# Recurrent front: the decay's inner product in columns 64 to 127 beside the mixer's second half, and keys projected a stage sooner

## The chip, the core and the metric

The kernel runs on one core of a Trainium2 chip. The metric is the device time of one launch in microseconds. A core has TensorE (matrix products into the accumulator memory PSUM), VectorE, ScalarE and GpSimd (elementwise work) and SyncE, which issues the transfers. Each has its own instruction queue and runs it in order; semaphores tie them together.

## The reference, cut to what matters

Four layers run one after the other on `x` of 4 samples x 512 tokens x 512 features, all in float32: a grouped attention over a context, a transformer block with self and cross attention and an MLP, and two recurrent layers (2 and 3) of one form. The change is in the first part of the recurrent layers:

```python
xa = _ln(x, ln1_w, ln1_b)
sx = concatenate([state[:, 1:2] - xa[:, :1], xa[:, :-1] - xa[:, 1:]], axis=1)
xxx = tanh((xa + sx * maa_x) @ maa_w1).reshape(b, l, 5, 32)     # the mixer: 512 -> 5*32
xxx = einsum('blfd,fde->blfe', xxx, maa_w2)                     # the mixings: 5 times 32 -> 512
xm = xa[:, :, None] + sx[:, :, None] * (maa_stack + xxx)
xk, xw, xv, xr, xg = (xm[:, :, j] for j in range(5))
w = exp(-exp(time_decay + tanh(xw @ td_w1) @ td_w2))            # the decay: 512 -> 64 -> 512
r, k, v = xr @ Wr.T, xk @ Wk.T, xv @ Wv.T
g = silu(xg @ Wg.T)
```

Then comes a recurrence over tokens (`s = k v + w s`), a group norm, an output product, and a feed-forward part.

## The kernel before

A loop runs over the four samples; all four layers of one sample are one body, each engine with a queue written out by hand. Features or tokens are tiled in four chunks of 128 (`C = 4`), tokens are 512 to a row. A recurrent layer has a front, which is what the reference's lines above say, then four rounds over the head groups (`hg`), then the output product and the feed-forward part. So there are eight fronts in a launch, two per sample.

The front on TensorE is in `pe_rwkv`. Its products are:

- `mixer(part, fc)` (L838): the mixer's product over input chunk `fc`. Part 0 gives 128 outputs (the tanh inputs of k, w, v, r, 32 each) into PSUM bank 0; part 1 gives the last 32 (g) into partitions 0 to 31 of bank 1.
- `decay_in(fc, mixed)` (L847): the decay's inner product, 64 outputs into bank 2. It is fed twice into the same sum, first by `xa` (`mixed=False`), then by `sx * (maa_w + xxx)` (`mixed=True`), so that xa needs not be added to the mixed w.
- `mixing(name, c)` (L858): one chunk of a 96-row product (32 values as high part, low part and high part again, in the format fp32r) for one of w, k, r, v, g. It writes into one of three PSUM banks, which mixings, decays and others take in turn (`take`): each use waits until the use three before it has been emptied.
- `project(0, name, fcs)` (L369): the projection of the first head group from mixed k, r or v, into the fixed banks 3, 7 and 2 (`FIRST`).
- the decay's outer product (L890): 64 rows to 128 outputs, four chunks, each into a bank of the three.

A product of float32 is recorded as two passes, one of fp32r as one.

The other engines follow the same order of names. ScalarE (`act_rwkv`) makes three tanh instructions per name w, k, r, v (L1363, L1364, L1366), then `tdh`, the tanh of the decay's inner product (L1386), then the three for g, then copies the first keys out of bank 3 (`kT`, L1375), and then makes two exponentials for each decay chunk (L1392, which empties the bank, and L1396). VectorE (`dve_rwkv`) empties each mixing with one instruction (L1126), adds `xa` to the last chunk of k, r and v (L1132), and makes the low part of each name's tanh (`z_low`, L1136); the low part for g comes after the last v. GpSimd adds `xa` to the other chunks (L1510), and later takes powers of the decay (L1520).

The weights come in blocks of 1 MB into three slots. A block may be loaded when its slot's block has been used for the last time. The block `small` holds the mixer's and both decay matrices and is free when the last L890 is done; the block of the values' weights goes into its slot (SyncE, `load_weights`, L278).

Of the kernel before, what the change touches and what calls it, by code (L numbers as in the profile page):

```python
# [16 lines left out]
ACT = mybir.ActivationFunctionType  # L17
# [4 lines left out]
C = H // P  # L22
# [26 lines left out]
SMALL_MAA, SMALL_TD1, SMALL_TD2 = 0, C * 160, C * 224  # L49
# [46 lines left out]
def build(nc, a, known, samples=B):  # L96
# [69 lines left out]
    tdh, over = place('tdh', [64, L], over)  # L166
# [46 lines left out]
    with ExitStack() as stack:  # L213
        ps = stack.enter_context(nc.psum_tensor('ps', [P, 8, 512], F32))
# [614 lines left out]
        def pe_rwkv(pe, l):  # L829
# [5 lines left out]
            def mixer(part, fc):  # L835
                n0, rows_ = ((0, 128), (128, 32))[part]
                pe.wait_ge(*dve_done.when('xin', l, fc))
                m = nc.tensor.matmul(ps[0:rows_, part, :], small[:, SMALL_MAA + fc * 160 + n0:SMALL_MAA + fc * 160 + n0 + rows_],  # L838
                                     mix[:, 1, fc, :], start=(fc == 0), stop=(fc == C - 1))
                if fc == C - 1:  # L840
                    m.then_inc(*tile_ready.reach('z', l, part))

            def decay_in(fc, mixed):
                src = mix[:, MIX_AT['w'], fc, :] if mixed else xa[:, fc, 1:L + 1]
                if mixed:
                    pe.wait_ge(*dve_emptied.when('mix', l, 'w', fc))
                m = nc.tensor.matmul(ps[0:64, 2, :], small[:, SMALL_TD1 + fc * 64:SMALL_TD1 + (fc + 1) * 64], src,  # L847
                                     start=(fc == 0 and not mixed), stop=(fc == C - 1 and mixed))
                if fc == C - 1 and mixed:
                    m.then_inc(*tile_ready.reach('td', l))  # L850

            def mixing(name, c):
                f = MIX_ROW[name]
                if c == 0:
                    pe.wait_ge(*dve_done.when('z_lo', l, name))
                    pe.wait_ge(*(act_emptied.when('z', l, int(f == 4)) if name in 'vg' else act_done.when('z_hi2', l, name)))
                tile = take(pe, 'mix', l, name, c)
                nc.tensor.matmul(tile, MIX_W[l][0:96, f * H + c * P:f * H + (c + 1) * P], zstack[0:96, f, :],  # L858
                                 start=True, stop=True).then_inc(*tile_ready.reach('mix', l, name, c))
# [8 lines left out]

            for fc in range(C):
                mixer(0, fc)  # L870
            decay_in(0, False)
            decay_in(1, False)
            pe.wait_ge(*(pool_done if l == 2 else dve_done).when('mix_w', l))
            for c in range(3):
                mixing('w', c)
            decay_in(2, False)
            mixing('w', 3)
            decay_in(3, False)
            for c in range(C):
                mixing('k', c)  # L880
                decay_in(c, True)
            for c in range(C):
                mixing('r', c)
                mixer(1, c)
            for c in range(C):
                mixing('v', c)
                project(0, 'k', (c,))
            pe.wait_ge(*act_emptied.when('td', l))
            for c in range(C):
                nc.tensor.matmul(take(pe, 'decay', l, c), small[0:64, SMALL_TD2 + c * P:SMALL_TD2 + (c + 1) * P], tdh[:, :],  # L890
                                 start=True, stop=True).then_inc(*tile_ready.reach('decay', l, c))
            for c in range(C):
# [460 lines left out]
        def act_rwkv(act, l):  # L1353
# [29 lines left out]
            for name in 'wkrv':  # L1383
                mixer_in(name)
            act.wait_ge(*tile_ready.when('td', l))
            nc.scalar.activation(tdh[:, :], ps[0:64, 2, :], ACT.Tanh).then_inc(*act_emptied.reach('td', l))  # L1386
            mixer_in('g')
            heads_in(0, 'k')
            for c in range(C + 1):
# [512 lines left out]
```

## Time and profile before

| | |
|---|---|
| median of three runs | 4186.95 us (4186.92 to 4193.72) |
| the profiled execution | 4188.31 us |
| its span, first to last instruction | 4186.5 us |
| mean granted TensorE clock | 0.952 |
| TensorE busy (weight loads, beside it) | 3719.4 us, 89% (2267.5 us, 54%) |
| VectorE busy | 2621.0 us, 63% |
| ScalarE busy | 2154.2 us, 51% |
| GpSimd busy | 1652.4 us, 39% |
| L838 (mixer), passes in all fronts | 128 |
| L847 (decay's inner product), passes | 128 |
| L858 (mixings), passes | 160 |
| L890 (decay's outer product), passes | 64 |

Busy shares are means over stages with different limits. The start of a pass on TensorE is recorded and its end is modelled, so the distance between starts is the measure of what a pass costs. Idle time in brackets is the idle time of the engine just before an instruction, with the instruction that ended it.

### The profile page before, as it was taken

To read this page: it belongs to the slowest core of one execution; us is meant where nothing else is said; L and a number is where in the kernel's file an instruction comes from. 1 tells how busy PE (TensorE), PEld (TensorE's weight loads), DVE (VectorE), ACT (ScalarE), POOL (GpSimd) and SP (SyncE) were. 2 spreads that over 40 slices of the span, in tenths; PEclk is the share of its full clock that TensorE was granted. 3 is DMA by queue.
4 is the path that set the end of the run, shared out by engine and by line. 5 is a ranking of instruction groups with operands and counts; after the bars stand their busy time and mean duration, and the time that the engine had idled before them with its cause. 6 is when DMAs were issued, how large, how long until landed. Compare 5 with 4: busy or idle time off the path is not lost. (4 is left out here: it accounts for less than half of the span.)

```text
span 4186.5 us, 66406 instructions
## 1 busy us (share of the span) xinstructions
PE 3719.4 (89%) x24448; PEld 2267.5 (54%) x24448; DVE 2621.0 (63%) x5691; ACT 2154.2 (51%) x4272; POOL 1652.4 (39%) x1849
## 2 busy tenths in 40 slices
PE   7988899899888989989888888998988888899898
PEld 4544565546554456554655445656465454565555
DVE  5765746666576564665657656467666765645766
ACT  5655733434666573343466657334346665733433
POOL 4554442232454454223245445422324544542232
PEclk9999999999999999999999999999999999999999
DMA  4032221102204122110220412211022032221102
GB/s 137 15 103 67 78 78 40 62 21 101 76 15 123 49 84 70 39 64 21 101 76 15 121 53 82 70 42 60 22 101 78 20 117 55 78 70 42 60 32 101
DMA packets 94558, 276.11 MB, mean 66 GB/s; under 512 B 25472, under 2 KB 25984, under 8 KB 73088
## 3 DMA queue, kind: packets, MB, share of 16 engines
q1 hardware_dynamic: 94208, 271.58, 20.2%
q8 instruction: 202, 3.31, 0.3%
q14 instruction: 148, 1.21, 0.1%
HBM read 201.24 MB, written 4.19 MB: 49 GB/s over the span
## 5 line engine op out<-in xcount | busy, mean ns | idle before, releaser
L805 POOL TENSOR_SCALAR probs<-probs,row_inv 128x512 f32<-128x512 f32 x1024 | 696.0, 696 | 635.1 <-DVE row_inv L720 635.1
L664 ACT ACTIVATE probs<-probs,row_max 128x512 f32<-128x512 f32 x1024 | 733.4, 725 | 132.1 <-DVE row_max L736 131.2
L559 PE MATMUL ps<-ident,probs 128*128 128x128 f32 x4096 | 606.5, 289 | 172.9 <-ACT pT L658 146.5
L559 PEld LDWEIGHTS ps<-ident,probs 128*128 128x128 f32 x4096 | 477.0, 146 | 383.0 <-ACT pT L658 211.4
L658 ACT ACTIVATE pT<-ps 128x512 f32<-128x512 f32 x768 | 430.1, 602 | 107.2 <-PE ps L559 106.5
L369 PE MATMUL ps<-mix,wring 128*128 128x512 f32 x1024 | 471.0, 596 | 3.8 <-DMA wring<-in_blocks_dram 3.8
L534 PE MATMUL ps<-kstack,qstack 96*128 96x512 f32 (+1 forms) x1024 | 380.5, 467 | 16.2 <-DMA qstack<-hi 7.1
L736 DVE CUSTOM_DVE_ANT_0 probs<-ps,maskA 128x512 f32<-128x512 f32 x512 | 329.3, 681 | 42.6 <-PE ps L534 42.6
L736 DVE CUSTOM_DVE_ANT_0 probs<-ps,neg 128x512 f32<-128x512 f32 x512 | 340.6, 685 | 8.9
L369 PEld LDWEIGHTS ps<-mix,wring 128*128 128x128 f32 x1024 | 191.2, 190 | 198.9 <-issue 178.8
L1535 POOL TENSOR_TENSOR hinv<-hvar,minus_half 128x32 f32<-128x32 f32 x24 | 146.3, 6094 | 376.8 <-DVE hvar L1255 376.8
L550 PE MATMUL ps<-pT,v 128*32 128x512 f32 x2048 | 244.6, 599 | 0.0
L369 PE MATMUL ps<-srcT,wring 128*128 128x512 f32 x512 | 238.5, 609 | 0.2
L534 PEld LDWEIGHTS ps<-kstack,qstack 96*128 96x128 f32 (+1 forms) x1024 | 177.1, 194 | 108.4 <-issue 44.1
L409 POOL TENSOR_SCALAR varep<-moments 128x1 f32<-128x1 f32 x128 | 43.0, 336 | 482.1 <-DVE moments L388 481.1
L329 POOL TENSOR_TENSOR mlp_w<-wring,mlp_w 128x2048 fp32r<-128x2048 f32 x32 | 149.5, 4672 | 194.2 <-ACT mlp_w L324 194.2
L421 PE MATMUL ps<-ident,xn 128*128 128x128 f32 x448 | 104.8, 389 | 126.6 <-DVE xn L392 126.1
L750 DVE COPY pT<-ps 128x512 f32<-128x512 f32 x256 | 168.2, 686 | 73.2 <-PE ps L559 71.7
L664 ACT ACTIVATION_READ_ACCUMULATOR probs<-probs,row_max 128x1 f32 x1024 | 205.4, 201 | 0.0
L1689 DVE TENSOR_TENSOR hidden_lo<-hidden,hidden_hi 128x512 fp32r<-128x512 f32 x64 | 94.2, 1495 | 168.7 <-ACT hidden_hi L1656 168.7
L1510 POOL TENSOR_TENSOR mix<-mix,xa 128x512 f32<-128x512 f32 x104 | 118.6, 1160 | 171.6 <-DVE mix L1126 122.4
L743 DVE TENSOR_TENSOR ps<-ps,maskA 128x1024 f32<-128x1024 f32 x128 | 156.5, 1223 | 23.1 <-PE ps L534 22.9
(177 smaller groups left out, 7025.9 us busy)
## 6 DMA issues: line engine op xcount, KB each, us to landing
wring<-in_blocks_dram SPq DMA_DIRECT2D x151, 1024.0 KB, 5.1
qstack<-hi SPq DMA_DIRECT2D x256, 64.0 KB, 2.0
kstack<-hi SPq DMA_DIRECT2D x256, 64.0 KB, 2.0
maskA<-in_mask_dram SPq DMA_DIRECT2D x9, 1024.0 KB, 7.8
rows<-in_rows_dram SPq DMA_DIRECT2D x8, 1024.0 KB, 4.6
qstack<-hi SPq DMA_DIRECT2D x256, 32.0 KB, 2.0
qstack<-lo SPq DMA_DIRECT2D x128, 64.0 KB, 2.0
kstack<-lo SPq DMA_DIRECT2D x128, 64.0 KB, 2.0
```

The source lines that it names most:

```text
L329: nc.gpsimd.tensor_tensor(low, weights(name), high.bitcast(F32), ALU.subtract).then_inc(*pool_done.reach('wlo', name))
L369: m = nc.tensor.matmul(tile, w[:, base_ + fc * H + oc * P:base_ + fc * H + (oc + 1) * P], src[:, fc, :], start=(fc == 0), stop=(fc == C - 1))
L534: nc.tensor.matmul(ps[:, qc, :], qstack[0:A.kt, g % 2, i, qc * P:(qc + 1) * P], kstack[0:A.kt, g % 2, 0 if A.shared else i, :], start=True ...
L550: ins = nc.tensor.matmul(ps[32 * h:32 * h + 32, OBANK, :], lhs, pT[:, h, kc, :], start=(kc == 0 and first), stop=(kc == C - 1 and final))
L559: ins = nc.tensor.transpose(tile[:, qc * P:(qc + 1) * P], probs[:, m % PSLOTS, qc, kc * P:(kc + 1) * P], ident[:, :])
L658: nc.scalar.activation(pT[:, m % 4, kc, :], ps[:, ring.bank('pT', t, m, kc), :], ACT.Copy)\
L664: nc.scalar.activation(p, p, ACT.Exp, bias=row_max[:, n % PSLOTS, qc:qc + 1], scale=-1.0, accum_out=row_sum[:, n % PSLOTS, qc:qc + 1]).the ...
L736: nc.vector.tensor_tensor_reduce(out=probs[:, s, qc, :], in0=ps[:, qc, :], in1=other, scale=-1.0, scalar=3.0e38, op0=ALU.add, op1=ALU.min, ...
L743: nc.vector.tensor_tensor(ps[:, two, :], ps[:, two, :], A.mask[:, two, :], ALU.mult)\
L750: nc.vector.tensor_copy(pT[:, m % 4, kc, :], ps[:, ring.bank('pT', t, m, kc), :])\
L805: nc.gpsimd.tensor_scalar(p, p, row_inv[:, (n - 1) % PSLOTS, qc:qc + 1], 1.0, ALU.mult, ALU.mult)\
L1535: nc.gpsimd.tensor_tensor(hinv[:, :, :], hvar[:, :, :], minus_half[:, :].rearrange('p (a b) -> p a b', b=HEADS), ALU.pow).then_inc(*pool_d ...
```

## The change

`decay_in` writes its 64 outputs to partitions 64 to 127 of bank 2, which puts the product in columns 64 to 127 of the array, where it was in columns 0 to 63. ScalarE reads them from there. The order on TensorE becomes:

- stage w: all of `mixer(1, fc)`, each followed by `decay_in(fc, False)`; then the four mixings of w with nothing between
- stage k: as it was, each mixing followed by `decay_in(c, True)`
- stage r: each mixing followed by one quarter of the first key projection (it was followed by `mixer(1, c)`)
- stage v: each mixing followed by one outer product of the decay (it was followed by a quarter of the key projection, with all outer products behind the stage); the wait for `tdh` stands behind the first v mixing
- stage g and the values' projection: as they were

The queues of VectorE, ScalarE, GpSimd and SyncE keep their order. The order in which banks are taken changes: v and decay chunks alternate.

```diff
-                m = nc.tensor.matmul(ps[0:64, 2, :], small[:, SMALL_TD1 + fc * 64:SMALL_TD1 + (fc + 1) * 64], src,
+                m = nc.tensor.matmul(ps[64:128, 2, :], small[:, SMALL_TD1 + fc * 64:SMALL_TD1 + (fc + 1) * 64], src,
                                      start=(fc == 0 and not mixed), stop=(fc == C - 1 and mixed))
...
             for fc in range(C):
                 mixer(0, fc)
-            decay_in(0, False)
-            decay_in(1, False)
+            for fc in range(C):
+                mixer(1, fc)
+                decay_in(fc, False)
             pe.wait_ge(*(pool_done if l == 2 else dve_done).when('mix_w', l))
-            for c in range(3):
+            for c in range(C):
                 mixing('w', c)
-            decay_in(2, False)
-            mixing('w', 3)
-            decay_in(3, False)
             for c in range(C):
                 mixing('k', c)
                 decay_in(c, True)
             for c in range(C):
                 mixing('r', c)
-                mixer(1, c)
+                project(0, 'k', (c,))
             for c in range(C):
                 mixing('v', c)
-                project(0, 'k', (c,))
-            pe.wait_ge(*act_emptied.when('td', l))
-            for c in range(C):
+                if c == 0:
+                    pe.wait_ge(*act_emptied.when('td', l))
                 nc.tensor.matmul(take(pe, 'decay', l, c), small[0:64, SMALL_TD2 + c * P:SMALL_TD2 + (c + 1) * P], tdh[:, :],
                                  start=True, stop=True).then_inc(*tile_ready.reach('decay', l, c))
...
-            nc.scalar.activation(tdh[:, :], ps[0:64, 2, :], ACT.Tanh).then_inc(*act_emptied.reach('td', l))
+            nc.scalar.activation(tdh[:, :], ps[64:128, 2, :], ACT.Tanh).then_inc(*act_emptied.reach('td', l))
```

## Rows read from the trace of the kernel before

**Rows 1.** Timeline of TensorE, first front: start us, us, instruction, idle.

```profile
612.77 1.93 PE L847 MATMUL ps<-xa,wring 128*64 128x512 f32 x4
614.82 0.94 PE L858 MATMUL ps<-zstack,mix_w 96*128 96x512 f32 x3
...
617.20 0.50 PE L858 MATMUL ps<-zstack,mix_w 96*128 96x512 f32 x1 [0.44 <-DVE mix L1126]
...
618.63 0.50 PE L858 MATMUL ps<-zstack,mix_w 96*128 96x512 f32 x1
...
623.37 1.07 PE L847 MATMUL ps<-mix,wring 128*64 128x512 f32 x2
624.37 0.50 PE L858 MATMUL ps<-zstack,mix_w 96*128 96x512 f32 x1
...
629.99 0.50 PE L858 MATMUL ps<-zstack,mix_w 96*128 96x512 f32 x1
...
630.79 0.80 PE L858 MATMUL ps<-zstack,mix_w 96*128 96x512 f32 x1
...
631.88 0.80 PE L858 MATMUL ps<-zstack,mix_w 96*128 96x512 f32 x1
...
633.61 1.02 PE L369 MATMUL ps<-mix,wring 128*128 128x512 f32 x2
634.57 3.88 PE L890 MATMUL ps<-tdh,wring 64*128 64x512 f32 x8
638.38 0.50 PE L858 MATMUL ps<-zstack,mix_w 96*128 96x512 f32 x1
...
641.99 1.02 PE L369 MATMUL ps<-mix,wring 128*128 128x512 f32 x2
643.58 3.70 PE L369 MATMUL ps<-mix,wring 128*128 128x512 f32 x8 [0.56 <-DMA wring<-in_blocks_dram]
```

**Rows 2.** Timeline of VectorE, first front.

```profile
616.40 2.73 DVE L1126 SCALAR_TENSOR_TENSOR mix<-ps,cols,sx 128x512 f32<-128x512 f32 x4
...
633.82 0.75 DVE L1126 SCALAR_TENSOR_TENSOR mix<-ps,cols,sx 128x512 f32<-128x512 f32 x1 [0.34 <-PE ps L858]
634.60 0.77 DVE L1132 TENSOR_TENSOR mix<-mix,xa 128x512 f32<-128x512 f32 x1
635.40 0.68 DVE L1136 TENSOR_TENSOR zstack<-z,zstack 32x512 fp32r<-32x512 f32 x1
638.91 0.75 DVE L1126 SCALAR_TENSOR_TENSOR mix<-ps,cols,sx 128x512 f32<-128x512 f32 x1 [2.83 <-PE ps L858]
```

**Rows 3.** Timeline of ScalarE, first front.

```profile
634.67 0.60 ACT L1375 ACTIVATE kT<-ps 128x512 f32<-128x512 f32 x1 [2.89 <-PE ps L369]
635.29 1.28 ACT L1392 ACT_TABLE_LOAD   x1
636.58 1.27 ACT L1392 ACTIVATE decay<-ps,cols 128x512 f32<-128x512 f32 x2
```

**Rows 4.** Windows, first and last front: length, busy of engines, clock, DMA share.

```profile
612.80:638.40 25.60, 25.05 (x58) 7.85 (x57) 17.12 (x24) 12.57 (x22) 10.23 (x9) 1.00 0.00 0
...
3971.00:3996.60 25.60, 25.03 (x58) 7.89 (x57) 17.10 (x24) 12.59 (x22) 10.23 (x9) 1.00 0.00 1
```

**Rows 5.** Chain that ended last (start us, us, what), one front; page's groups.

```profile
3766.06 3.82 PE ps L890 x8
3769.90 5.07 DMA wring<-in_blocks_dram
...
L369 PE MATMUL ps<-mix,wring 128*128 128x512 f32 x1024 | 471.0, 596 | 3.8 <-DMA wring<-in_blocks_dram 3.8
```

**Rows 6.** Timeline of TensorE in an attention: a context group, what follows.

```profile
3269.41 1.92 PE L550 MATMUL ps<-pT,v 128*32 128x512 f32 x16
3271.26 0.33 PE L559 MATMUL ps<-ident,probs 128*128 128x128 f32 x1
```

**Rows 7.** Timeline of GpSimd, first front.

```profile
620.70 3.44 POOL L1510 TENSOR_TENSOR mix<-mix,xa 128x512 f32<-128x512 f32 x3 [11.23 <-DVE mix L1126]
```

## The prediction

> **What bounds the kernel now.** I read the table of slices and the list of groups first. No engine is full: TensorE is busy for 89% of the span, and what the program waits for differs from stage to stage. The change touches one stage only, the front of the two recurrent layers (from the layer norm's transposes to the projection of values), which runs eight times: four samples, two layers. So the view to read is the timeline of TensorE over one front [rows 1], beside those of VectorE [rows 2] and ScalarE [rows 3] over the same stretch, and the table of windows that says whether the other fronts are like it. They are: in the first and in the last of the eight, TensorE is busy for 25.0 of 25.6 us at a granted clock of 1.00, with VectorE at 17.1 and ScalarE at 12.6 us, and no DMA runs [rows 4]. A front is bound by TensorE's queue as it is ordered, and what is taken off that queue counts, until a wait shows up in its place.
>
> The chain of work that ended last confirms the end of a front: four outer products of the decay (L890), then a weight load of 5.07 us, then the projection of values [rows 5]. That load brings the values' block into the slot of the small block, which is free only when the last L890 has read it. TensorE reaches the projection first: it could go on at 642.85 (641.99 plus two passes of 0.43) and starts at 643.58 [rows 1]. Over all fronts the group of projections has 3.8 us idle for this load [rows 5]. A record of a pass is 0.59 long and passes follow each other at 0.43, so 0.16 per front is hidden in that idle time: 3.8/8 + 0.16 = 0.64 us per front are lost here.
>
> **The prices on TensorE.** A float32 product of 512 columns is two passes of 0.43 us, 0.86 in all (L369 x8 takes 3.70 us with its tail) [rows 1]. From the same timeline: a turn of "one mixing, one decay input" takes (624.37 - 618.63)/4 = 1.43 us, of which the 64-column product is 1.00 (623.37 to 624.37) and the mixing 0.43. A turn of "one mixing, one mixer second half" takes (629.99 - 624.37)/4 = 1.41. A turn of "one mixing, one projection" takes only 631.88 - 630.79 = 1.09, though its product is as long [rows 1]. So 0.3 us of a turn is paid for going between full-width products and products of 64 or 32 columns.
>
> **The change part by part.** I write the first front as a schedule; its start, 612.77, stays.
>
> (1) Stage w. Removed: four decay inputs on xa alone or between the w mixings. Added: four second halves of the mixer, each followed by a decay input in other columns. What four products in disjoint columns do is seen in the attention's context: sixteen passes (eight products) of 32 columns take 3271.26 - 3269.41 = 1.85 us [rows 6], where one after another they would take 8 x 0.86 = 6.9. So disjoint columns work at the same time. No row shows a 32-column product beside a 64-column one. Bounds for a pair: 0.86 (beside each other) and 2.00 (two of the alternating ones at 1.00 [rows 1]). I take 0.86, since every row with disjoint columns is at that end. Four pairs are 3.45, with 0.1 for going back to full width: w0 at 616.3, where it was at 614.82.
>
> VectorE now ends this stage. The mixings take turns on three PSUM banks, so w3 waits until VectorE has emptied w0, and k0 until it has emptied w1. Its read begins 0.53 after a mixing starts (638.38 to 638.91) and takes 0.68 (2.73/4) [rows 1, 2]. The signal back takes 0.12 (616.40 + 0.68 to 617.20): 616.3 + 0.53 + 1.36 + 0.12 = 618.3 for k0, before 618.63. The decay inputs that used to fill this wait had cost nothing there, so this step gives 0.3 us and no more; four mixer halves are now inside it.
>
> (2) Stage k is unchanged in TensorE's order, 4 x 1.43: r0 at 624.1. The other columns cost the decay inputs nothing, and ScalarE's tanh reads 64 partitions as before.
>
> (3) Stage r pairs each mixing with a k projection. By the present v stage that is 0.80 for the first turn (629.99 to 630.79) and 1.09 for the others [rows 1], 4.07 in all, against 5.62 now: v0 at 628.2. The projection needs mixed keys a stage earlier: VectorE reads them from 616.85 + 2.73 + 0.7 = 620.3 on (r's low part stands between), GpSimd adds xa at 1.15 us each (3.44/3) [rows 7], and the last is there by 624.8, before its projection at 627.7. The keys' weights have landed: no DMA runs from 612.80 on [rows 4].
>
> (4) Stage v alternates mixings with L890. No row shows this pair. The nearest is 1.43 (64 columns); an L890 loads weights for 128 columns on each change, so I take 1.47, with 1.09 and 1.6 as bounds. The wait for `tdh`, now behind the first v mixing, costs nothing: its input ends with stage k at 624.1, four us earlier. The first L890 starts at about 628.9, behind the last k projection; v1 at 630.0, v2 at 631.45, v3 at 632.9. Three banks now turn among mixings and decays, so v2 waits for ScalarE to empty decay 0, v3 for decay 1. ScalarE: the tanh for g finds its input early and is out of the way; the last k projection starts 0.45 before v0 and takes 1.02 [rows 1], so kT starts at 628.8, then the 1.28 of its table load and 0.69 for the exponential, in the order and with the times of now [rows 3]: 628.8 + 0.6 + 1.28 + 0.69 = 631.35. That is 0.1 before v2 wants it: a cover with nothing to spare. If it is late by x, v2, v3 and g0 are late by x.
>
> (5) A new wait. VectorE reads v3 at 632.9 + 0.53 = 633.45 (now 633.82), adds xa and makes g's low part, which ends at 635.40 + 0.68 = 636.08 now, 2.26 after that read began [rows 2]: at 635.7, and g0 follows at 635.85. The last L890 ends near 634.4. Four L890 used to stand between v3 and g0 and hid this; now TensorE stands for some 1.4 us, with the projection of receptance behind it in its queue. g0 comes 638.38 - 635.85 = 2.5 us sooner.
>
> (6) Stage g is unchanged, 642.85 - 638.38 = 4.47: the projection of values may start at 640.3. The small block is free at 634.4 and the 5.07 us of the load end at 639.5, so SyncE's load is hidden and the 0.64 us is saved as well. What follows (vT, pair products, decay powers on GpSimd) moves with it: VectorE's products hang on the projection of receptance, which moves by 2.5, and reach their next TensorE user with more than 3.2 - 2.5 to spare.
>
> **Sum**: 2.5 + 0.64 = 3.15 us per front, 25.2 us for eight. The profiled execution took 4188.31 us, 1.8 more than its span; less 25.2 it is 4163.1. The median of the runs is 4186.95, 1.36 less, so I say 4161.8.
>
> **The rivals.**
>
> Rival A, the pair does not run side by side and each change of width is paid. For it: the trace pays 0.3 us per turn whenever widths alternate [rows 1], and 32 and 64 are different widths. Against it: the widths that were seen to pay share columns, and these don't. Then a pair costs 2.00, four cost 8.0 in place of 3.45, everything behind moves by 4.55, and a front is 4.55 - 3.15 = 1.4 us longer: +11.2 us, 4198.2. It decides as soon as a pair costs more than 0.86 + 3.15/4 = 1.65 us. 
>
> Rival C, side by side, but ScalarE or VectorE hands back the banks late in stage v. If decay 0 waits for the whole table load after it is ready (630.0 + 1.28 + 0.69 = 632.0), v2 is 0.6 late and so is g0: 2.55 us per front, 20.4 in all, 4166.6. Against it: the load now starts at 635.29, straight behind kT and before the decay is there [rows 3].
>
> **How the numbers follow.** The forecast, with the pairs side by side, 0.50; Rival C 0.08; Rival B 0.12; Rival A 0.30. The range takes in the forecast with cheap L890 turns (1.3 in place of 1.47 gives 0.5 us a front, 4158; with the rest of the roundings 4156) and Rival A, with 2 us of spread: 4156 to 4200. The forecast's own range is 4156 to 4168. About 0.2%, 8.4 us, is what a measurement of this kernel can tell from no change. Faster: forecast and C, 0.58. Same: B and a fifth of A, where a change of width costs less than at full width, 0.18. Slower: the rest of A, 0.24.
>
> **What the profile afterwards would show.** Step 1: L838 with 32 columns and L847 with 64 start within some 0.02 us of each other, the eight products take about 3.5 us, and k0 follows w0 by 2.0. If they start 0.43 apart or more and take 7 to 8 us, A or B holds. Steps 3 and 4: turns of 1.09 and 1.47. Step 5: a wait of VectorE's zstack in front of the first g mixing, 1 to 1.5 us. Step 6: no idle time for wring before the projection of values. I would be wrong, beyond the rivals, if the new wait in front of g0 let the granted clock fall below 1.00 inside a front, or if what follows a front did not move with it.

## The result, and the profile after

The change made the kernel slower: 4208.85 us (median of 7 runs, 4203.77 to 4227.76) against 4186.95 (7 runs beside them, 4180.48 to 4197.67), a ratio of 1.006 with a 95% interval of 1.0047 to 1.0072. The profiled execution took 4208.85 us, its span is 4207.1 and its mean granted clock 0.950. The forecast was 4161.8, so it had the sign wrong, and the range ended at 4200.

All that follows rests on one table. The start of each pass on TensorE cuts a front into stages; these are the means of the eight fronts of a profiled execution, in us. "To w0" is the time from the last pass of the mixer's first half to the first mixing of w, "end" that from the last mixing of g to the first product that transposes v.

| kernel | to w0 | w | k | r | v | g | end | sum |
|---|---|---|---|---|---|---|---|---|
| before | 2.57 | 3.82 | 5.72 | 5.61 | 8.37 | 2.98 | 6.52 | 35.58 |
| after | 8.44 | 2.09 | 5.70 | 4.07 | 7.88 | 4.36 | 5.78 | 38.31 |

A front grew by 38.31 - 35.58 = 2.73 us, eight of them by 21.8; the spans differ by 4207.1 - 4186.5 = 20.6. So the loss is as large as the growth of the fronts; some microseconds elsewhere are taken up at the end. Every stage behaved alike in all of them but stage g, which is treated below.

The timeline of TensorE in the first front of the kernel after (columns as in [rows 1]) shows what the pairs did:

```profile
613.53 1.57 PE L838 MATMUL ps<-mix,wring 128*128 128x512 f32 x3
...
615.46 1.07 PE L847 MATMUL ps<-xa,wring 128*64 128x512 f32 x2
616.47 1.05 PE L838 MATMUL ps<-mix,wring 128*32 128x512 f32 x2
617.44 1.07 PE L847 MATMUL ps<-xa,wring 128*64 128x512 f32 x2
...
621.40 1.07 PE L847 MATMUL ps<-xa,wring 128*64 128x512 f32 x2
622.40 0.97 PE L858 MATMUL ps<-zstack,mix_w 96*128 96x512 f32 x3
...
624.49 0.48 PE L858 MATMUL ps<-zstack,mix_w 96*128 96x512 f32 x1 [0.25 <-DVE mix L1123]
...
630.20 0.49 PE L858 MATMUL ps<-zstack,mix_w 96*128 96x512 f32 x1
...
634.27 0.80 PE L858 MATMUL ps<-zstack,mix_w 96*128 96x512 f32 x1
635.00 1.12 PE L887 MATMUL ps<-tdh,wring 64*128 64x512 f32 x2
636.05 0.50 PE L858 MATMUL ps<-zstack,mix_w 96*128 96x512 f32 x1
...
637.53 0.49 PE L858 MATMUL ps<-zstack,mix_w 96*128 96x512 f32 x1
...
639.44 1.12 PE L887 MATMUL ps<-tdh,wring 64*128 64x512 f32 x2
642.15 0.50 PE L858 MATMUL ps<-zstack,mix_w 96*128 96x512 f32 x1 [1.58 <-DVE zstack L1133]
642.48 1.87 PE L369 MATMUL ps<-mix,wring 128*128 128x512 f32 x2
643.37 1.42 PE L858 MATMUL ps<-zstack,mix_w 96*128 96x512 f32 x1
...
646.79 0.80 PE L858 MATMUL ps<-zstack,mix_w 96*128 96x512 f32 x1
647.43 4.46 PE L369 MATMUL ps<-mix,wring 128*128 128x512 f32 x10
```

The 64-column product and the 32-column product never share a row or a start. They follow each other at 1.01 and 0.97 us, so a pair takes 617.44 - 615.46 = 1.98, and the mixings of w begin at 622.40. Behind them the rest of the schedule is nearly as forecast, up to the wait of 1.58 us in front of the first mixing of g. Behind that wait stands something new: a pass of L858 of 1.42 us, and a whole stage of 646.79 - 642.15 = 4.64 us where the same instructions took 2.98.

The windows over stage g (length, busy of TensorE, its weight loads, VectorE, ScalarE and GpSimd, granted clock, DMA share, GB/s) of the first, second, sixth and eighth front say why:

```profile
642.15:646.80 4.65, 4.65 (x10) 2.35 (x10) 1.77 (x3) 0.18 (x1) 0.10 (x1) 0.63 0.47 194
869.03:874.70 5.67, 5.67 (x9) 2.84 (x10) 2.08 (x3) 0.17 (x1) 0.09 (x1) 0.51 0.41 168
...
2965.30:2968.30 3.00, 3.00 (x10) 1.66 (x10) 1.78 (x3) 0.18 (x1) 0.10 (x1) 1.00 0.75 311
...
4013.41:4016.40 2.99, 2.99 (x10) 1.66 (x10) 1.77 (x3) 0.18 (x1) 0.10 (x1) 1.00 0.79 326
```

TensorE is busy throughout, with the same work, and the granted clock is 0.63 and 0.51 in the long ones and 1.00 in the short ones. It fell to 1.2 GHz, half of full speed, for most of stage g in six of the eight fronts, and cost 1.66 us in five of them and 2.70 in the second.

### The profile page after: what moved, and what is told of

It reads as the page before. It is cut to its first block and busy times, and to the rows that moved or that the text cites. A ratio compares the mean times of both kernels' runs of the same rounds, so it can differ in the third digit from the quotient of the medians.

```text
span 4207.1 us, 66406 instructions
## 1 busy us (share of the span) xinstructions
PE 3734.0 (89%) x24448; PEld 2270.7 (54%) x24448; DVE 2623.0 (62%) x5691; ACT 2155.6 (51%) x4272; POOL 1655.9 (39%) x1849
## 3 DMA queue, kind: packets, MB, share of 16 engines
q8 instruction: 202, 3.31, 0.3%
```

## The experiments

Two questions stood open: what a pair costs and why, and what the wait in front of g does. A third came up on the way: TensorE's stops in the recurrence, which moved whenever instructions were added. Each run's stages are gathered in one table behind the first group.

### What the pair costs

Only the width of one product decides in this run: the mixer's second half is made 64 columns wide (the 32 added outputs land in partitions that nobody reads), so that both products of a pair are of one width.

```diff
-                n0, rows_ = ((0, 128), (128, 32))[part]
+                n0, rows_ = ((0, 128), (128, 64))[part]
```

> The changed kernel with one edit: the mixer's second half takes 64 columns of weights in place of 32 (columns 0 to 63 of the array; the upper 32 results are never read). Both products of a pair are then 64 wide, in columns 0 to 63 and 64 to 127, with their banks and operands as they were. Theory M (what keeps a pair apart is that 32 and 64 columns are two widths, and each change of width drains the array): the pairs run side by side, 0.86 us a pair, from the last pass of the mixer's first half to w0 8.44 falls to about 4.0 us; k0, r0, v0, g0 move with it, so 4.4 us per front, 35 us in all, near 4173 us. Theory N (a product of the mixer and one of the decay don't overlap because they read different operands or write different banks): 8.44 stays within 0.8 us of what it is (the changes of width alone are saved), at most 6 us in all.

It took 4177.75 us (12 runs), ratio 0.9979 (0.9966 to 0.9992) to before, 31.1 us below after. The timeline of TensorE, first front:

```profile
616.10 0.59 PE L838 MATMUL ps<-mix,wring 128*64 128x512 f32 x1
616.11 0.59 PE L847 MATMUL ps<-xa,wring 128*64 128x512 f32 x1
616.53 0.59 PE L838 MATMUL ps<-mix,wring 128*64 128x512 f32 x1
616.54 0.59 PE L847 MATMUL ps<-xa,wring 128*64 128x512 f32 x1
```

The two products start 0.01 us apart, and the next pair of passes follows 0.43 later: side by side at last, with more work than before. "To w0" fell from 8.44 to 4.11.

In the next run the columns overlap again: the decay goes back to columns 0 to 63, while the change's order stays.

```diff
-                m = nc.tensor.matmul(ps[64:128, 2, :], small[...], src,
+                m = nc.tensor.matmul(ps[0:64, 2, :], small[...], src,
```

> The changed kernel with the decay's inner product back in columns 0 to 63 (partitions 0 to 63 of bank 2), the order on TensorE as changed. Theory M: since 32 and 64 wide products drain each other anyway, the columns make no difference: 8.44 us from the mixer's first half to w0, the same time as the changed kernel within 0.1 us per front. If instead the disjoint columns bought any overlap, this is longer by it.

4215.61 us (5 runs), ratio 1.0067 (1.0045 to 1.009). "To w0" is 8.44, the same to a hundredth. With widths of 32 and 64, having the columns apart bought nothing.

Then the same eight products with one change of width among them instead of seven: four mixer halves, then four decay inputs.

```diff
             for fc in range(C):
                 mixer(1, fc)
+            for fc in range(C):
                 decay_in(fc, False)
```

> The changed kernel with the four mixer halves first and then the four decay inputs on xa, in place of alternating: one change of width where there were seven. Theory M: each change costs about 0.12 us over the 0.86 of a product ((1.98 - 1.72)/2), so 6 x 0.12 to 0.14 = 0.8 us less: 8.44 falls to 7.6 us; 6 us less in all. If a pair were kept apart by something that is not the change of width, alternating and grouped would take the same.

4207.17 us (8 runs), ratio 1.0048 (1.003 to 1.0067). The timeline of TensorE, first front:

```profile
617.64 3.65 PE L847 MATMUL ps<-xa,wring 128*64 128x512 f32 x8
621.22 0.97 PE L858 MATMUL ps<-zstack,mix_w 96*128 96x512 f32 x3
```

Seven of the eight passes of the decay follow the one before at 0.43 to 0.48, and "to w0" is 7.66. So most of the loss is that the products stand one after the other; the changes of width add 8.44 - 7.66 = 0.78 us, 0.13 for each of the six that were taken out.

The last of this group makes all parts 32 wide: each decay input as two products of 32 columns, at 64 and 96, beside the mixer's 32.

```diff
-                m = nc.tensor.matmul(ps[64:128, 2, :], small[..., 64 columns], src, ...)
+                for h in range(2):
+                    m = nc.tensor.matmul(ps[64 + 32 * h:96 + 32 * h, 2, :], small[..., 32 columns], src, ...)
```

> The changed kernel with each decay input split into two products of 32 columns, in columns 64 to 95 and 96 to 127, with the mixer's half in 0 to 31: three products of one width, four more than before in count and the same work. Theory M: one width, three places, so all three run side by side in stage w: 8.44 falls to about 4.1 us although there are 12 products in place of 8. In stage k the two halves run side by side, a turn stays at 1.43. About 35 us less in all. Theory N: twelve products one after another, 8.44 grows by 4 x 0.86 to about 11.5 us (minus the changes of width), unless only the two decay halves overlap, which leaves it near 7.4.

4142.58 us (4 runs), ratio 0.9901 (0.9876 to 0.9927). The timeline of TensorE, first front (L848 is the decay's line here):

```profile
618.00 0.59 PE L838 MATMUL ps<-mix,wring 128*32 128x512 f32 x1
618.01 0.60 PE L848 MATMUL ps<-xa,wring 128*32 128x512 f32 x2
618.43 0.59 PE L838 MATMUL ps<-mix,wring 128*32 128x512 f32 x1
```

Three passes start within a few hundredths and the next three 0.43 later: three products abreast, "to w0" 4.09, and each decay input costs the same in two parts as in one (stage k 5.61 against 5.70). But the kernel is 35 us faster than the one with 64 columns, whose fronts are as long. Neither theory had that; it is the subject of the third group.

The stages of all kernels that are told here:

| kernel | to w0 | w | k | r | v | g | end | sum | stops |
|---|---|---|---|---|---|---|---|---|---|
| before | 2.57 | 3.82 | 5.72 | 5.61 | 8.37 | 2.98 | 6.52 | 35.58 | 14 |
| after | 8.44 | 2.09 | 5.70 | 4.07 | 7.88 | 4.36 | 5.78 | 38.31 | 12 |
| e1_wide64 | 4.11 | 2.09 | 5.69 | 4.07 | 7.88 | 4.67 | 5.81 | 34.33 | 14 |
| e2_overlap | 8.44 | 2.09 | 5.69 | 4.07 | 7.88 | 4.49 | 5.78 | 38.44 | 13 |
| e3_grouped | 7.66 | 2.09 | 5.69 | 4.07 | 7.88 | 4.48 | 5.80 | 37.66 | 15 |
| e4_three32 | 4.09 | 2.09 | 5.61 | 4.07 | 7.88 | 4.69 | 5.81 | 34.24 | 2 |
| e5_g_sooner | 8.44 | 2.09 | 5.70 | 4.07 | 9.66 | 5.06 | 5.78 | 40.80 | 13 |
| e8_three32_g_sooner | 4.09 | 2.09 | 5.61 | 4.07 | 10.22 | 4.53 | 5.78 | 36.39 | 2 |
| e9_filled | 8.44 | 2.09 | 5.69 | 4.07 | 7.88 | 3.05 | 5.78 | 37.00 | 9 |
| e10_low_parts_early | 4.09 | 5.02 | 9.21 | 4.07 | 6.23 | 2.98 | 6.30 | 37.91 | 2 |
| e13_low_parts_placed | 4.09 | 3.31 | 6.41 | 4.07 | 6.97 | 3.83 | 6.12 | 34.80 | 3 |
| e14_no_waits | 4.09 | 2.09 | 5.62 | 4.07 | 7.34 | 4.25 | 6.08 | 33.54 | 2 |
| e7_before_split | 2.56 | 3.80 | 5.64 | 5.61 | 8.37 | 2.98 | 6.31 | 35.27 | 2 |
| e11_before_padded | 2.56 | 3.82 | 5.71 | 5.60 | 8.37 | 2.98 | 6.38 | 35.43 | 2 |
| e12_after_padded | 8.44 | 2.09 | 5.69 | 4.07 | 7.88 | 4.55 | 5.78 | 38.50 | 0 |
| e15_before_pad16 | 2.56 | 3.82 | 5.71 | 5.61 | 8.37 | 2.98 | 6.31 | 35.36 | 6 |
| e16_before_pad64 | 2.57 | 3.81 | 5.71 | 5.60 | 8.37 | 2.98 | 6.30 | 35.36 | 4 |

"Stops" counts the idle times above 0.4 us of TensorE, over the launch, for which the trace shows no wait.

### What the wait in front of g costs

Two products of 128 columns that nobody reads are put between the last L887 and the first mixing of g, behind two waits that were long met. They do nothing but keep TensorE at work.

```diff
+            w_wait(pe, f'r_{l}')
+            pe.wait_ge(*act_emptied.when('z', l, 1))
+            for n in range(2):
+                nc.tensor.matmul(ps[:, 1, :], weights(f'r_{l}')[:, 0:P], xa[:, n, 1:L + 1], start=True, stop=True)
```

> The changed kernel with two products of no use (1.7 us, into bank 1, which is free then) between the last outer product of the decay and the first g mixing. The wait there is filled with work, nothing comes sooner. Theory W: the clock stays at 1.00 in stage g, 2.98 us in all fronts, and each front is 1.4 us shorter for more work done: 10 us less. Rival (not the standing still): stage g stays at 4.4 us on average and the time of the changed kernel stays or grows.

4186.14 us (10 runs), ratio 1.0 (0.9989 to 1.001) to before: useless work won 22.7 us over after. The windows over stage g, first two fronts and the sum of all eight:

```profile
641.80:644.90 3.10, 3.10 (x11) 1.77 (x10) 1.81 (x3) 0.18 (x1) 0.10 (x1) 1.00 0.73 304
864.84:867.90 3.06, 3.06 (x11) 1.73 (x10) 1.76 (x3) 0.18 (x1) 0.11 (x1) 1.00 0.77 319
...
sum 24.39, PE 24.39 PEld 13.73 DVE 14.04 ACT 1.44 POOL 0.82; mean PE 3.05 PEld 1.72 DVE 1.76 ACT 0.18 POOL 0.10
```

The clock is 1.00 in every one, and the sum is 24.39 us. The same sum of the kernel after:

```profile
sum 34.92, PE 34.91 PEld 17.89 DVE 14.80 ACT 1.44 POOL 0.79; mean PE 4.36 PEld 2.24 DVE 1.85 ACT 0.18 POOL 0.10
```

Stage v is 7.88 in both, so g starts no sooner; only the clock has changed. That is 1.31 us a front, 10.5 in all. The other half of the 22.7 is not in the fronts; three stops fewer (12 to 9) would be about 9 of it by the third group.

The other profiled kernels say the same. Six have this wait of 1.58 us in all their fronts (after, e1, e2, e3, e4 and e12), and stage g takes 4.44 us or more in 37 of their 48 fronts and 2.98 or 2.99 in the rest. Five have the order of before and no such wait (before, e7, e11, e15 and e16), and there it is 2.98 in all 40.

The other way to be rid of the wait is to make g's low part sooner: ScalarE makes g's tanh before the decay's, VectorE the low part before it reads v.

```diff
-            mixed('v')
             z_low('g')
+            mixed('v')
...
-            for name in 'wkrv':
+            for name in 'wkrvg':
...
-            mixer_in('g')
```

> The changed kernel with g's three tanh instructions in front of the one for `tdh` on ScalarE, and g's low part in front of the four v reads on VectorE (it stood behind them). The wait of 1.6 us in front of the first g mixing has no cause left. Theory W (the granted clock fell to 0.5 in stage g of 6 of 8 fronts because TensorE stood before it): the g mixings take 2.98 us from first to last in all eight fronts, as in the kernel before, in place of 4.36 on average. The first g mixing comes 1.65 us sooner, less some 0.4 for the low part that now delays the first v read. In all 8 x (1.2 + 1.4) = 21 us less than the changed kernel, near 4188 us. Rival (the clock falls there for another reason, the load that starts at the same time or the many changes of width in stages w to v): the wait goes, the clock still falls in most fronts, 10 us less.

4234.49 us (4 runs), ratio 1.010 (1.0076 to 1.0123): a miss, by 46 us. VectorE, GpSimd and TensorE in the first front:

```profile
636.38 1.65 DVE L1133 TENSOR_TENSOR zstack<-z,zstack 32x512 fp32r<-32x512 f32 x1
...
633.62 3.86 POOL L1506 TENSOR_TENSOR mix<-mix,xa 128x512 f32<-128x512 f32 x3 [2.12 <-DVE mix L1123]
...
638.87 1.12 PE L887 MATMUL ps<-tdh,wring 64*128 64x512 f32 x2 [1.45 <-DVE mix L1123]
```

The low part, 0.68 us in [rows 2], takes 1.65 here, of which 1.10 stand beside GpSimd's sums, which end at 637.48. The banks of v come free that much later, and TensorE waits 1.45 us in front of the second L887. The wait had only moved, and the clock fell in stages v and g.

The next four runs start from the kernel with three products of 32. The first has the two edits just shown.

> Both cures in the changed kernel: three products of 32 columns side by side in stage w, and g's tanh and low part sooner. If the two add up as theory M and theory W have it: 4142 us (the first alone) less some 1.2 us for the wait and 1.5 for the clock per front, 21 us: near 4120 us, 1.6% faster than before. If VectorE is now the bound in stage v, the wait moves in front of the v or decay products and half of it stays: 4130.

4155.99 us (5 runs), ratio 0.9918 (0.9904 to 0.9932), a miss too: stage v 10.22 and g 4.53, 13.4 us worse than without the edits. The second keeps ScalarE's new order and makes the first four low parts at once, and g's before the mixed keys:

```diff
-            z_low('w')
-            z_low('k')
+            for name in 'wkrv':
+                z_low(name)
             mixed('w')
-            z_low('r')
-            mixed('k')
-            z_low('v')
-            mixed('r')
-            mixed('v')
             z_low('g')
+            for name in 'krv':
+                mixed(name)
```

> Three products of 32 columns side by side in stage w, and all low parts made where neither a mixing waits for VectorE nor GpSimd works: those of w, k, r, v before the w reads, that of g behind them; g's tanh before `tdh`. In the variant with g's low part in front of the v reads, that instruction took 1.65 us in place of 0.68 beside GpSimd's sums, v0 was emptied late, and the wait moved from the first g mixing to the second outer product of the decay (1.45 us). Theory (it was the place, not the idea): no wait over 0.5 us from v0 to g0, g0 follows v0 by 6.3 us in place of 7.88; the clock stays at 1.00 in stage g, 2.98 us in all eight fronts. Against the three-product variant alone (4142 us): 8 x (1.6 + 1.6) = 26 us less, near 4117, 1.7% faster than before. Rival (stage v is bound by VectorE whatever the order): another wait takes its place and the time stays at 4140 to 4156.

4160.99 us (6 runs), ratio 0.9938 (0.9917 to 0.996). TensorE, first front:

```profile
622.15 1.52 PE L860 MATMUL ps<-zstack,mix_w 96*128 96x512 f32 x2 [3.31 <-DVE mix L1125]
```

Stages v and g came out as wished, 6.23 and 2.98. But VectorE stood for ScalarE's tanh of v before it read the first w, so the fourth w mixing waited 3.31 us for its bank, and the clock fell in stage k: 9.21 us for instructions that take 5.61. The third has the low parts of v and g between the reads of w and k:

```diff
-            for name in 'wkrv':
+            for name in 'wkr':
                 z_low(name)
             mixed('w')
-            z_low('g')
+            for name in 'vg':
+                z_low(name)
```

> As the last variant with early low parts, but v's low part behind the w reads: VectorE makes those of w, k, r, then the four w reads, then the low parts of v and g, then the reads of k, r, v. In the last variant VectorE stood until ScalarE had made v's tanh (620.63) with w0 waiting; the w reads began late, k0 followed w0 by 5.02 us in place of 2.09, and the clock fell in stage k of 7 of 8 fronts (9.7 us in place of 5.6). Theory (each wait of over some 1.4 us of TensorE in a front costs itself and a stretch at half clock; without one the front runs at 1.00): k0 2.1 us after w0, stage k 5.6, g0 6.2 after v0, stage g 2.98, in all eight fronts: a front of 31.3 us from the mixer's first half to the first product on values, where the kernel before has 35.6. With the two stops of the three-product variants: near 4115 us, 1.7% faster than before. Rival: with the reads of k 0.7 us later the ring of banks holds up stage k, a wait of over 1 us shows there and the clock falls again: 4130 to 4145.

4140.42 us (4 runs), ratio 0.9886 (0.9868 to 0.9904), against 4115 hoped for. TensorE, first front:

```profile
619.72 0.50 PE L860 MATMUL ps<-zstack,mix_w 96*128 96x512 f32 x1 [1.60 <-DVE mix L1125]
```

Now VectorE stood for r's tanh, and the fourth w mixing waited 1.60 us for its bank, in all eight fronts. The clock fell in stage k behind it in four of them, and in stages v or g in three of the others. The fourth gives each low part the place at which its tanh is there (the edit is shown against the kernel after; ScalarE's order stays as in the last three):

```diff
             z_low('r')
-            mixed('k')
             z_low('v')
+            mixed('k')
+            z_low('g')
             mixed('r')
             mixed('v')
-            z_low('g')
```

> Three products of 32 columns side by side in stage w, g's tanh before `tdh`, and VectorE's order: low parts of w, k, the w reads, low parts of r, v, the k reads, low part of g, the r and the v reads. In the last variant VectorE stood for ScalarE's r tanh (618.21) with w0 made at 617.16, so w3 waited 1.60 us and the clock fell in stage k of four fronts; in the other four it fell in stage v or g. Here nothing made by ScalarE after k's tanh stands in front of the w reads. Theory (the clock falls where TensorE stood for over 1.2 us just before, and only there): stage w to k 2.1, stage k 5.6, g0 6.2 after v0, stage g 2.98, in all eight fronts; against the last variant 8 x (1.2 + 0.8 + 0.7 + 0.85) = 28 us, with some 0.6 us a front given back to the load of the values' weights: 4115 to 4122 us. Rival (the clock falls for something else in stages w to v, such as the amount of work in narrow columns): no wait, but the clock still falls in some fronts, 4125 to 4140.

4129.06 us (5 runs), ratio 0.9866 (0.9843 to 0.9889): the fastest of all, 1.3% faster than before. From the first mixing of w to the last of g no wait exceeds 0.38 us. And still the clock fell in four of the eight fronts, so the theory of this run, that it falls only behind a wait, failed; the time is in the rival's 4125 to 4140. The windows over stage v of the third, fifth and sixth front, and TensorE in the fifth:

```profile
1662.40:1668.30 5.90, 5.61 (x13) 1.75 (x12) 4.11 (x7) 4.88 (x7) 5.90 (x6) 1.00 0.01 3
2685.20:2693.10 7.90, 7.63 (x12) 2.14 (x11) 4.64 (x7) 4.87 (x7) 6.85 (x8) 0.72 0.00 0
2907.40:2915.60 8.20, 7.91 (x13) 2.25 (x12) 4.63 (x7) 4.88 (x7) 6.91 (x8) 0.69 0.00 1
...
2687.05 1.12 PE L889 MATMUL ps<-tdh,wring 64*128 64x512 f32 x2 [0.27 <-DVE mix L1125]
2688.52 1.96 PE L889 MATMUL ps<-tdh,wring 64*128 64x512 f32 x2
```

The pass at 2688.52 is drawn out to half speed with nothing but an idle time of 0.27 us ahead. So a wait is not needed for the clock to fall, though a wait of 1.6 us was enough in six fronts of eight, and to fill it was enough to stop that. What else the chip goes by stays open.

### The stops in the recurrence

Far from the front, in the recurrence, TensorE runs groups of 128 products of 32 x 32 over 128 columns (`v_blocks` by `k_tok`, L966 in before). The timeline of before shows one of them broken:

```profile
709.85 1.72 PE L966 MATMUL ps<-v_blocks,k_tok 32*32 32x128 f32 x108
713.50 0.47 PE L966 MATMUL ps<-v_blocks,k_tok 32*32 32x128 f32 x20 [1.93 <-issue]
```

"Issue" is idle time for which the profile shows no wait. Where there is no stop, the group passes in one piece, as in the kernel of the next run (timeline of TensorE):

```profile
712.30 1.89 PE L968 MATMUL ps<-v_blocks,k_tok 32*32 32x128 f32 x128
```

That run changes nothing of the order of before: each decay input is only written as two products of 32 columns, at 0 and 32. It asks whether the 35 us come with the number of instructions ahead of the recurrence or with something of the change.

```diff
-                m = nc.tensor.matmul(ps[0:64, 2, :], small[..., 64 columns], src, ...)
+                for h in range(2):
+                    m = nc.tensor.matmul(ps[32 * h:32 * h + 32, 2, :], small[..., 32 columns], src, ...)
```

> The kernel before with one edit: each decay input as two products of 32 columns, side by side in columns 0 to 31 and 32 to 63. Order and places stay. In a front it can change next to nothing (a turn of stage k was 1.43 with 64 columns and 1.40 with twice 32). It asks where the 35 us went that the three-product variant of the changed kernel has over the one with 64 columns, with equal fronts: in that variant TensorE's stops in the 128 small products of the later rounds (L966 here, 1.5 to 2.2 us each, released by nothing in the trace, with a fall of the clock behind them) were 2, where all others have 12 to 14. Theory P (the place in the instruction stream: 32 more TensorE instructions per front in front of those products move where fetching breaks off): here too the stops go to a few, and the kernel is 25 to 40 us faster than before, near 4155 us. Rival (it is the order of the changed kernel, or fewer changes of width): 14 stops remain and the time is that of before within 5 us.

4143.08 us (4 runs), ratio 0.9888 (0.9872 to 0.9903). The fronts are 35.27 against 35.58, 2.5 us in all; the other 41 go with 12 stops. So the gain of the kernel with three products of 32 over its sister had little to do with columns.

The next adds nothing but place: eight products of 8 columns per front, whose result nobody reads, ahead of before's mixer.

```diff
+            for n in range(8):
+                nc.tensor.matmul(ps[0:32, 1, 0:8], small[:, 0:32], small[:, 0:8], start=True, stop=True)
             for fc in range(C):
                 mixer(0, fc)
```

> The kernel before with eight products of 8 columns and no use at the start of each front (32 TensorE instructions per front, as many as splitting the decay inputs adds, and about 0.5 us of work). Nothing else is touched. Theory P (the place of the instructions decides where fetching breaks off in the 128 small products of the later rounds): the stops there go from 14 to about 2, and the time is 4186 - 43 + 4 = about 4147 us. Rival (the split products themselves do it): 14 stops, about 4191 us.

4151.84 us (4 runs), ratio 0.992 (0.9893 to 0.9946). The fronts are 35.43 us against 35.58, and the stops 2 in place of 14.

The same eight products go into the kernel after, at the same place:

> The changed kernel with the same eight useless products. If the cost of the change (22 us) lies in the fronts alone, it is still 22 us slower than the kernel before with the same padding, and both have about 2 of the stops: near 4169 us. If part of the cost was in the stops, the two stand closer.

4167.27 us (6 runs), ratio 0.9952 (0.9931 to 0.9973), no stop at all, fronts of 38.50. With the stops all but gone on both sides, the change costs 4167.27 - 4151.84 = 15.4 us: 8 x (38.50 - 35.43) = 24.6 for the fronts, less some 6 for the two stops that are left in before's padded form, would be 18.6. The slowest of before's padded runs, 4160.93, is below the fastest of after's, 4164.99, but both spread over some 10 us, so the 15.4 is rough. Last, half the padding and twice the padding in before:

```diff
-            for n in range(8):
+            for n in range(4):      # and range(16)
```

> The kernel before with four useless products of 8 columns per front in place of eight: 16 TensorE instructions more. Theory P (place in the instruction stream): the count of stops in the 128 small products is a function of the shift; it was 14 at 0 and 2 at 32, so between them at 16, with a time between 4152 and 4187 us. If the stops depended on the kind of work, they would be 2 here as well.

> The kernel before with sixteen useless products per front: 64 TensorE instructions more. Theory P: another place again; if what matters is where a fetched piece of the stream ends against the small products, the stops may come back (5 to 14), although more instructions stand in front. If more instructions were simply better, 0 to 2 stops.

One run each, 4168.11 and 4156.12 us. The idle time by cause of the line with the products, from the view of that line (us, times), for before, its pad of four products, its pad of eight, and the other group of 128 products (L986) under the pad of sixteen:

```profile
  issue: 52.9, 28
...
  issue: 24.8, 12
...
  issue: 7.5, 4
...
  issue: 24.5, 25
```

A stop is counted there twice, for the product and for its weight load; the last row holds small idle times besides. Four products leave 6 stops of 14, eight leave 2, and sixteen leave none on this line but 4, of 1.8 to 2.3 us, on the other group. Four products gave a count and a time between those of none and eight, as expected. Sixteen brought stops back, but 4 and not 5 to 14. So the stops hang on where these instructions lie in the stream, not on what is computed. Their price, from three comparisons: with the fronts' part taken off, 34 us go with 12 stops between the kernels with 64 and with 32 columns, 41 with 12 in the split one, 34 with 12 in the padded one. That is some 3 us each, though the idle time itself is 24.5 us for 14, 1.75 each. A part of the rest is the clock behind them; a window of before over one stop and what follows has the clock at 0.79 though TensorE is idle for less than 2 us of 8:

```profile
3842.00:3850.00 8.00, 6.09 (x103) 3.03 (x91) 1.59 (x3) 1.11 (x1) 5.75 (x2) 0.79 0.04 16
```

The Trainium skill, "Runtime: NRT & Kernel Launch", Instruction fetch mechanics, says that instructions are fetched in blocks of 256 and that this is mostly hidden. The trace has these blocks: packets of 16384 bytes that the profile calls "instruction", 202 on queue 8 in every kernel here. This is the line for queue 8 in the view of DMA queues of before, over the window 710.7 to 712.2:

```profile
q8 instruction: 1, 0.02, 5.4%
```

That packet was under way from 710.79 to 712.08, and TensorE went on at 713.50, 1.42 us after it. So it is with all 115 stops in the 17 profiles: each ends 1.2 to 1.6 us after the end of such a packet and 2.2 to 2.9 after its start, though the stops themselves last 0.5 to 2.3 us. In before all fourteen begin behind the 106th, 108th, 122nd or 124th product of a group. A group is 128 products and their weight loads, 256 instructions in 1.9 us, which is shorter than those 2.2 to 2.9. "Mostly hidden" agrees: 202 packets in before and 14 stops. Such packets also come during groups that don't stop, and no run changed the fetching alone; so fetching as the cause rests on this timing and on the dependence on place, and was not shown by an experiment of its own.

## Why the prediction was wrong

**Step 1 failed**, and its failure is the sign. The pair was taken at 0.86 us, "since every row with disjoint columns is at that end". Those rows, the attention's context [rows 6], have disjoint columns and equal widths; the pair has disjoint columns and unequal ones. It measured 1.98, the upper bound of 2.00. Equal widths gave the 0.86 that was hoped for (4.11 us to w0, where the prediction's schedule has 4.05). The argument against Rival A, that the widths seen to pay share columns, took the wrong property of the rows: sharing columns made no difference at all (8.44 both ways). Rule and rows now agree on this: what the Trainium skill says under "TensorEngine Tiling (Array Packing)", Key Properties, of draining on a change of mode holds between 32 and 64 columns.

**The terms that held.** k0 came 2.09 after w0 (2.0), stage k is 5.70 (4 x 1.43), stage r 4.07 (4.07). A turn with L887 takes 637.53 - 636.05 = 1.48 (1.47). ScalarE's cover of 0.1 us for v2 was there, as its timeline shows:

```profile
636.78 0.69 ACT L1389 ACTIVATE decay<-ps,cols 128x512 f32<-128x512 f32 x1
```

It ends at 637.47, and v2 starts at 637.53, so Rival C's case did not come up. The load of the values' weights is hidden, and the end of the front is 6.52 - 5.78 = 0.74 shorter (0.64).

**The wait in front of g** was named, with 1.4 us, and measured 1.58. The chain on VectorE:

```profile
639.55 0.75 DVE L1123 SCALAR_TENSOR_TENSOR mix<-ps,cols,sx 128x512 f32<-128x512 f32 x1 [0.73 <-PE ps L858]
640.34 0.95 DVE L1129 TENSOR_TENSOR mix<-mix,xa 128x512 f32<-128x512 f32 x1
641.32 0.77 DVE L1133 TENSOR_TENSOR zstack<-z,zstack 32x512 fp32r<-32x512 f32 x1
```

From the read of v3 to the end of the low part it is 642.09 - 639.55 = 2.54, where it was 2.26: the add is 0.95 in place of 0.77 and the low part 0.77 in place of 0.68, both beside GpSimd, which makes the powers of the decay at that time (L1517, 640.13 to 642.25); in before it stood idle from 634.82 to 638.44. The prediction took over the 2.26 without asking what would then run beside it.

**What the wait did** was not in the sum. The fall of the clock stood among what would make the prediction wrong, without price or chance, and it came: 4.36 - 2.98 = 1.38 us per front. The account per front: 5.87 to w0, -1.73 in w, -0.02 in k, -1.54 in r, -0.49 in v, +1.38 in g, -0.74 at the end, in all +2.73. Without the clock it is +1.35, and Rival A said +1.4. So Rival A was right in its mechanism and to the tenth in its price, and the range was too short at the top because a term outside both stories was left out of it. Rival A's 4198.2 and 8 x 1.38 of the clock make 4209.2, where 4208.85 was measured; that they meet so closely is luck, by what stays open below.

**What stays open.** The spans grew by 20.6 us and the fronts by 21.8, though two stops fewer should have given some 6 back; some 5 us of the launch are not located. That is less than the spread of either kernel's runs (17 us before, 24 after). What the chip goes by when it lowers the clock without a wait is open, and so is why the same wait lowered it in some fronts and not in others. The stops agree with the fetching of instructions in their timing, which no run tested by itself.

## What to carry to other kernels

Products in disjoint columns ran abreast here where their widths were equal, and 32 beside 64, the one unequal pair that was run, did not. So write a 64-column product as two of 32 beside a 32-column one, or widen the narrow one; both cost nothing here. When a reordering opens a wait on TensorE, price the clock behind it as well as the wait, and if nothing useful can fill it, filling it uselessly may still pay. Compare two versions only after looking at the stops far from the edit, since eight tiny products moved this kernel by 35 us, more than the change itself.

## What the runs showed of the hardware that was not expected

- 32 and 64 columns apart in the array: 1.98 us a pair; 64 and 64: 0.86; 32, 32 and 32: 0.86. A change between 32 and 64 costs 0.13 us. The 0.3 us of a turn between full width and 64 or 32 [rows 1] is for two changes, so a change has about the same price there.
- With a wait of 1.58 us in front of stage g the clock fell to 1.2 GHz in that stage in six of eight fronts, which cost 1.66 us in five and 2.70 in one; with the wait filled, in none. With no wait over 0.38 us (e14_no_waits) it still fell in four of eight.
- VectorE's low part of 0.68 us took 1.65 beside GpSimd's sums, and GpSimd's three sums 3.86 in place of 3.44 [rows 7]. The Trainium skill, "SBUF — State Buffer", SBUF: two separate sides, says that a VectorE instruction with two SBUF inputs and a GpSimd one lock a shared port pair against each other; the longer times agree. No run tested this by itself.
- Fourteen stops of 1.4 to 2.2 us in groups of small products, some 3 us each with what follows; four or eight products ahead of each front left 6 or 2. All 115 stops in the 17 profiles end 1.2 to 1.6 us after the end of a 16384-byte packet of instructions.
